# A mixture-of-experts feed-forward in one core: the first product by a seven-multiplication block scheme, with the hidden rows written to memory and read back by a second phase

## What is computed

```python
h = jax.lax.ragged_dot(x_rep_sort, w1, group_sizes)
h = jax.nn.silu(h) * jax.lax.ragged_dot(x_rep_sort, w3, group_sizes)
out_sort = jax.lax.ragged_dot(h, w2, group_sizes)
...
out = jnp.einsum('tkd,tk->td', out_rep, topk_w)
return out.reshape(b, s, d)
```

## Time and profile before

| | |
|---|---|
| three timed runs | 8394.23, 8397.29, 8398.87 us (median 8397.29) |
| profiled execution | 8408.29 us, its span 8406.7 us |
| PE busy | 8220.8 us, 98% |
| DVE busy | 3531.5 us, 42% |
| ACT busy | 3267.5 us, 39% |
| POOL busy | 478.6 us, 6% |
| bytes moved | 1189.77 MB, 142 GB/s over the span |

### The profile page before, as it was taken

How to read it: one execution, slowest core, us unless ns; L and a number is a source line. 1 busy time by engine, 2 the same in 40 slices (tenths; PEclk the granted TensorE clock), 3 DMA queues, 4 the chain that set the end, 5 groups by cost and what they waited for, 6 DMA issues and landing times.

```text
span 8406.7 us, 119512 instructions
## 1 busy us (share of the span) xinstructions
PE 8220.8 (98%) x46092; PEld 7566.7 (90%) x46093; DVE 3531.5 (42%) x3602; ACT 3267.5 (39%) x3511; POOL 478.6 (6%) x580
## 2 busy tenths in 40 slices
PE   8959999999999999999999999999999999999998
PEld 5549999999999999999999999999999999999998
DVE  6755333443443334453333334453333334433343
ACT  2325333443333334453333334453333333433343
POOL 2320000000000000000000000000000000000000
PEclk8969999999999999999999999999999999999999
DMA  3335444553443434553434434554434344444343
GB/s 113 115 111 185 142 135 135 179 162 131 139 149 122 147 120 151 169 185 120 141 129 134 141 128 150 161 187 142 135 130 139 120 145 141 152 143 135 130 154 116
DMA packets 839095, 1189.77 MB, mean 142 GB/s; under 512 B 27872, under 2 KB 722400, under 8 KB 839072
## 3 DMA queue, kind: packets, MB, share of 16 engines
q1 hardware_dynamic: 812096, 1116.05, 40.5%
q0 software_dynamic: 26976, 73.42, 3.7%
HBM read 1121.90 MB, written 71.67 MB: 142 GB/s over the span
## 4 chain that ended last, share of the span: by engine, by line
PE 92%; ACT 0%; issue 0%; DVE 0%; DMA 0%; ACTq 0%; POOL 0%; POOLq 0%; DVEq 0%
PE p L1038 20%; PE p L1040 20%; PE p L1039 20%; PE acc L1063 10%; PE acc L1064 10%; PE acc L1062 10%; PE p L1093 1%; DVE lo L975 0%; ACT hi L921 0%; ACT L921 0%; DMA out_x<-y,id_s 0%; DMA xg<-x_rows,id_g 0%; DVE xlo L1001 0%; ACT xhi L946 0%; ACT y L963 0%
## 5 line engine op out<-in xcount | busy, mean ns | idle before, releaser
L1038 PE MATMUL p<-xhi,hi 128*128 128x384 f32 (+4 forms) x10752 | 3435.3, 320 | 30.6 <-DVE lo L975 19.1
L1040 PE MATMUL p<-xhi,lo 128*128 128x384 f32 (+4 forms) x10752 | 3432.7, 319 | 0.0
L1039 PE MATMUL p<-xlo,hi 128*128 128x384 f32 (+4 forms) x10752 | 3430.0, 319 | 0.0
L1038 PEld LDWEIGHTS p<-xhi,hi 128*128 128x128 f32 x10752 | 2029.1, 189 | 65.7 <-issue 41.3
L1039 PEld LDWEIGHTS p<-xlo,hi 128*128 128x128 f32 x10752 | 2030.5, 189 | 24.3
L1040 PEld LDWEIGHTS p<-xhi,lo 128*128 128x128 f32 x10752 | 2028.1, 189 | 0.0
L988 DVE TENSOR_TENSOR hid<-sil,p 128x384 f32<-128x384 f32 x672 | 372.4, 554 | 3764.0 <-PE p L1040 3764.0
L975 DVE TENSOR_TENSOR lo<-raw,hi 128x2048 fp32r<-128x2048 f32 x673 | 1543.4, 2293 | 792.8 <-ACT hi L921 792.8
L1062 PE MATMUL acc<-hi,hhi 128*128 128x512 f32 x3808 | 1497.6, 393 | 0.0
L1064 PE MATMUL acc<-hi,hlo 128*128 128x512 f32 x3808 | 1491.5, 392 | 0.0
L1063 PE MATMUL acc<-lo,hhi 128*128 128x512 f32 x3808 | 1490.6, 391 | 0.0
(11 more groups left out here) (181 smaller groups left out, 2439.4 us busy)
## 6 DMA issues: line engine op xcount, KB each, us to landing
raw<-in_L_ffn_w SPq DMA_DIRECT2D x1011, 1024.0 KB, 5.1
xin<-in_x SPq DMA_DIRECT2D x8, 2048.0 KB, 10.7
out_x<-x SPq DMA_DIRECT2D x32, 512.0 KB, 2.9
x_rows<-x SPq DMA_DIRECT2D x32, 512.0 KB, 3.7
ctxt<-in_ctx SPq DMA_DIRECT2D x4, 1024.0 KB, 9.6
table<-rec,posi POOLq DMA_INDIRECT x80
xg<-x_rows,id_g POOLq DMA_INDIRECT x75, 6.7
out_x<-y,id_s POOLq DMA_INDIRECT x72, 7.3
```

What stands on the lines that cost most here:

```text
L1038: pe.matmul(bank[:, 0:n], hi13[par][:, a, k, :], xhi[:, k, 0:n], start=(k == 0), stop=False)
L1039: pe.matmul(bank[:, 0:n], hi13[par][:, a, k, :], xlo[:, k, 0:n], start=False, stop=False)
L1040: mm = pe.matmul(bank[:, 0:n], lo13[par][:, a, k, :], xhi[:, k, 0:n], start=False, stop=(k == KT - 1))
```

## The change

`experts` is rewritten. A slot is now up to 1024 rows of one expert (HALF = 512), cut into an even half and an odd half of equal width n; n is rounded up to one of WIDTHS. An expert whose count needs an odd number of 512s starts with a slot of 512 rows. With the counts above there are 12 slots: two with n = 496, two with n = 512, and eight narrow ones (experts 2, 4, 6 and 7 have two each): four with n = 256, three with 272, one with 288.

**First phase.** 28 units per slot: a unit is one matrix (w1, then w3) for two tiles of hidden columns. Cut in 2 by 2 blocks (two tiles by two halves of k, and two halves of k by two halves of the rows), it takes seven products instead of eight, each of 4 steps of k with three matmuls of n columns: 84 matmuls. For that, four sums of weight blocks are formed by POOL for every unit (`weight_sums`, into `sums`), four sums of row blocks once per slot (`row_sums`), and DVE combines the products from four banks into four results (`unit`), since the banks are used again within the unit. ACT and DVE split seven weight operands of 512 columns per unit (`weight_hi`, `weight_lo`). The hidden values of a pair go to a tensor `hd` in memory (1 MB per pair of tiles).

**Second phase.** After the 28 units, four passes c over the 28 tiles: one half of the rows (nh) by one half of the output columns (dh). Here w2 is stationary and the hidden values are moving, n columns at a time. A step is two tiles: SP loads 512 KB of w2 and 512 KB of `hd`, ACT and DVE split both, PE does 24 matmuls. 56 steps per slot; w2 and `hd` are read twice each in this way. Between steps t+5 and t+6 of a pass PE turns the results of the pass before back (`turn_back`, 16 transposes) and turns a quarter of the next slot's rows (`turn_rows`, 16 transposes). ACT, DVE and POOL have the copies for these in their queues.

In narrow slots ACT and DVE work on 288 columns (NARROW) where they otherwise work on 512. `raw13[1]` serves in the second phase as the second buffer of w2 and `hd`.

The diff, cut to its core:

```diff
+HALF = 512
+KH = KT // 2
+EP = 7
+PAIRS = MT // 2
+UNITS2 = 2 * PAIRS
+WIDTHS = (256, 272, 288, 384, 496, 512)
+NARROW = 288
...
-                sp.wait_ge(s_lo13, s * MT + pair * 2 - 1)
-                sp.dma_start(raw13[parity][:, 0], w1v[bass.ds(e, 1), :, :, bass.ds(pair * 2 * P, 2 * P)].rearrange(
...
+            def load_down(e, c, i, par):
+
+                nh, dh = c // 2, c % 2
+                sp.dma_start(raw2[par], w2v[bass.ds(e, 1), :, bass.ds(i * 2, 2), dh * HALF:(dh + 1) * HALF].rearrange(
+                    "e p m d -> (e p) m d")).then_inc(s_raw2[par], 16)
+                sp.dma_start(rawh[par], hdv[nh, :, bass.ds(i * 2, 2), :]).then_inc(s_rawh[par], 16)
+
+            def store_hidden(s, i):
+
+                sp.wait_ge(s_hid, s * (PAIRS * 3) + i * 3 + 3)
+                sp.dma_start(hd[bass.ds(i * 4, 4)].rearrange("q p n -> p q n"), hid[:, :, :]).then_inc(s_hst, 16)
...
+                                sp.wait_ge(s_w2lo, s * STEPS + c * PAIRS + i2 * 2 + par + 1)
+                                sp.wait_ge(s_hlo, s * STEPS + c * PAIRS + i2 * 2 + par + 1)
+                                load_down(e, c, i2 * 2 + par, par)
...
+            def down_hi(s, t, cols):
+
+                par = t % 2
...
+                act.wait_ge(s_down, s * (STEPS * 4) + 4 * t + 4)
+                act.wait_ge(s_raw2[par], s * (STEPS * 8) + (t // 2) * 16 + 16)
+                copy(wh[:, 4 * par:4 * par + 2, :], raw2[par]).then_inc(s_w2hi, 1)
+                act.wait_ge(s_rawh[par], s * (STEPS * 8) + (t // 2) * 16 + 16)
+                copy(wh[:, 4 * par + 2:4 * par + 4, 0:cols], rawh[par][:, :, 0:cols]).then_inc(s_hhi, 1)
...
+                after(3)
+                product_done(s, i, a, 4)
+                plus(v[:, 0:cols], s1[:, 0:cols], b2[:, 0:cols]).then_inc(s_v, 1)
+                dve.wait_ge(s_v, g + 2)
+                plus(to[:, 3, 0:cols], v[:, 0:cols], b4[:, 0:cols]).then_inc(s_c22, 1)
+                after(4)
+                if a == 1:
+                    dve.wait_ge(s_c22, g + 1)
+                    gate(3, 1)
+                product_done(s, i, a, 5)
+                plus(to[:, 1, 0:cols], v[:, 0:cols], b5[:, 0:cols]).then_inc(s_c12, 1)
+                after(5)
+                if a == 1:
+                    dve.wait_ge(s_c12, g + 2)
+                    gate(1, 2)
+                product_done(s, i, a, 6)
+                dve.wait_ge(s_u2, g + 1)
+                plus(to[:, 2, 0:cols], u2[:, 0:cols], b4[:, 0:cols]).then_inc(s_c21, 1)
+                after(6)
...
+                    for k in range(KH):
+                        ks = slice(k * P, (k + 1) * P)
+                        pe.matmul(o, wh[:, e, ks], xh[:, e, k, 0:n], start=begin and k == 0, stop=False,
+                                  skip_group_check=True)
+                        pe.matmul(o, wh[:, e, ks], xl[:, e, k, 0:n], start=False, stop=False, skip_group_check=True)
+                        mm = pe.matmul(o, wl[:, e, ks], xh[:, e, k, 0:n], start=False, stop=k == KH - 1,
+                                       skip_group_check=True)
...
+                pe.wait_ge(s_c11, g + 1)
+                product(0, b1, True)
+                pe.wait_ge(s_c21, g + 1)
+                product(1, b4, True)
+                pe.wait_ge(s_v, g + 1)
+                product(2, b2, True)
+                pe.wait_ge(s_s1, g + 1)
+                product(3, b1, False)
+                pe.wait_ge(s_u2, g + 1)
+                product(4, b2, False)
+                pe.wait_ge(s_c12, g + 1)
+                product(5, b5, True)
+                pe.wait_ge(s_c22, g + 1)
+                product(6, b4, False)
...
+                free(1)
+                G.tensor_tensor(sums[:, 0, :, :], A11, A21, ALU.subtract).then_inc(s_sum, 1)
+                free(4)
+                G.tensor_tensor(sums[:, 1, :, :], A21, A22, ALU.add).then_inc(s_sum, 1)
+                pool.wait_ge(s_sum, done + 2)
+                free(2)
+                G.tensor_tensor(sums[:, 2, :, :], sums[:, 1, :, :], A11, ALU.subtract).then_inc(s_sum, 1)
+                pool.wait_ge(s_sum, done + 3)
+                free(5)
+                G.tensor_tensor(sums[:, 3, :, :], A12, sums[:, 2, :, :], ALU.subtract).then_inc(s_sum, 1)
```

More of the change, by code:

```diff
@@ L697, in by_slot @@
                 return a[0:1, :].unsqueeze(1).to_broadcast([1, META, E])
-            s_i, mine, i_in, start, t_a, t_b = (sl[:, i, :, :] for i in range(6))
+            s_i, mine, start, t_a, t_b = (sl[:, i, :, :] for i in range(5))
             step(V.tensor_copy(s_i, sidx[:, :, :]))
@@ new lines, in copy, with weight_hi @@
+            def copy(out, in_, scale=1.0):
+                return nc.scalar.activation(out, in_, ACT.Copy, scale=scale)
+            def weight_hi(s, i, a, e, fresh=False, first=False):
+                if first:
+                    pass
+                elif fresh:
+                    act.wait_ge(s_down, s * (STEPS * 4) + (4 if e < 4 else 8))
+                else:
+                    act.wait_ge(s_prod, s * PRODUCTS + i * (2 * EP) + a * EP + e + 1)
+                if e == 0:
+                    act.wait_ge(s_raw13[a], s * (PAIRS * 16) + i * 16 + 16)
+                if e in SUM_OF:
+                    act.wait_ge(s_sum, s * (PAIRS * 8) + i * 8 + a * 4 + SUM_OF[e] + 1)
+                copy(by_k(wh[:, e, :]), weight_part(a, e)).then_inc(s_whi, 1)
@@ new lines, in quad, with rows_hi @@
+            def quad(n, q, first=False):
+                act.wait_ge(s_xt, n * 4 + q + 1)
+                if not first:
+                    act.wait_ge(s_xlo, n * EP)
+                copy(quads[:, q, :, :], by_k(bank[q][:, :])).then_inc(s_quad, 1)
+            def rows_hi(n, c, i):
+                e, q, ready = X_PARTS[i]
+                if ready:
+                    act.wait_ge(s_xsum, n * 4 + ready)
+                else:
+                    act.wait_ge(s_quad, n * 4 + q + 1)
+                copy(xh[:, e, :, c * P:(c + 1) * P], quads[:, q, :, :]).then_inc(s_xhi, 1)
@@ new lines, in _ @@
+            act.wait_ge(s_clear, 1)
+            for e in range(EP):
+                weight_hi(0, 0, 0, e, first=True)
+            for c in range(4):
+                if c == 0:
+                    act.wait_ge(s_wlo, EP)
+                for q in range(4):
+                    quad(c, q, first=c == 0)
+                for i in range(EP):
+                    rows_hi(c, c, i)
+            with act.Fori(0, SLOTS) as s:
+                width = slot_value(act, 2, s, N8_MOST)
+                with act.If(width > 0):
+                    with act.If(width > NARROW // 8):
+                        slot(s, HALF)
+                    with act.Else():
+                        slot(s, NARROW)
+                    act.nop()
@@ new lines, in _ @@
+            dve.wait_ge(s_raw13[0], 16)
+            less(sums[:, 0, :, :], A11, A21).then_inc(s_sum, 1)
+            plus(sums[:, 1, :, :], A21, A22).then_inc(s_sum, 1)
+            dve.wait_ge(s_sum, 2)
+            less(sums[:, 2, :, :], sums[:, 1, :, :], A11).then_inc(s_sum, 1)
+            dve.wait_ge(s_sum, 3)
+            less(sums[:, 3, :, :], A12, sums[:, 2, :, :]).then_inc(s_sum, 1)
+            for e in range(EP):
+                weight_lo(0, 0, 0, e)
+            for c in range(4):
+                for i in range(EP):
+                    rows_lo(c, c, i)
@@ L1055, in hidden @@
[L1055 removed]
+                        between(lo, half)
+                between(0, len(WIDTHS) - 1)
                 pe.nop()
[L1058 to L1064 removed]
@@ L1205, in moe_kernel @@
+            tick(0)
+            for c in range(4):
+                gather(c, first_x[2 * c:2 * c + 2], s_xfirst[c])
+            for c in range(4):
+                row_sums(c)
+            pool.wait_ge(s_xlo, 4 * EP)
+            weight_sums(0, 0, 1)
+            with pool.Fori(0, SLOTS) as s:
+                width = slot_value(pool, 2, s, N8_MOST)
+                with pool.If(width > 0):
+                    slot(s, width)
+                pool.nop()
 def moe_kernel(nc, x, ctx_in, W_k, b_k, gamma, beta, gate_w, w1, w2, w3, out):
```

864 lines of the change are left out of this document (546 added, 318 removed).

## The result

The changed kernel takes **9136 us** (median of 4 runs, 9135.2 to 9146.3), the kernel before 8398 in the same session: a ratio of **1.088**, 95% interval 1.086 to 1.090. It is slower, as forecast, but by 8.8% and not by 1.4%: the time lies outside of the range of 8060 to 8950.

What follows compares the result with a forecast made beforehand. PE's matmuls were taken to bound the kernel. Span 8407 - 694 + 159 + 22 = 7894, plus 254 (first phase), 276 (second phase) and 100 (clock) = 8524; forecast 8515 us, 1.4% slower, range 8060 to 8950.

Steps and rivals of the forecast that it cites:

- PE's work, minus 694: PE's matmuls in both phases: first phase 623 us less, second phase 72 us less.
- First phase, DVE and POOL, plus 254: Narrow first-phase units: DVE and POOL delay each other, so PE waits; 234 us narrow, 20 wide, at 1.1 us per sum.
- the exclusion: First phase: DVE operations with both inputs in SBUF and POOL's sums block each other; 234 us in narrow slots.
- Second phase, plus 276: Second-phase loads: 3.4 us per step against PE's 2.9 in narrow slots; 260 us narrow, 16 wide, range 0 to 736.
- Clock, plus 100: PE's granted clock falls after pauses, with 60 seams and many short waits; 100 us, range 0 to 250.
- Seams, plus 159: Transposes and waits between steps and at slot ends: 22 us per slot, 264 in all, for 105 before.
- start, plus 22: Kernel start: 1024 rows to gather, turn, sum and split before the first product; 22 us on top of 39.
- The covers hold: Faster rival: DVE and POOL do not hold each other up, loads keep pace; about 8060 us, chance 0.25.
- POOL's sum at IOTA's rate: Slower rival: first-phase POOL sums of 2.1 us make narrow units 13.8 us; around 9000 us, chance 0.11.
- The loads collide: Slower rival: second-phase loads delay each other, 4.3 us per step, DMA share above 0.9; 9000 us, chance 0.05.

Runs made afterwards that it cites:

- e1: Changed kernel with POOL's four weight sums per unit working on one element instead of 512 (stale sums, waits kept); 8848 us, 1.053.
- e16: e13 with high parts first in the first phase too (8648 us), and DVE's two weight sums moved to the start of the unit before; 8504 us.
- e9: Changed kernel with SP's waits parted in the second phase: w2 and hidden-row loads each wait only for their own half of the buffer; 9034 us.
- e2: Changed kernel with SP issuing second-phase loads of steps 2 to 7 before waiting for the last hidden store and loading next weights; 9054 us.
- e13: e12 with PE's eight high-part products first in each second-phase step, then the sixteen with low parts; 8650 us, 1.029.
- e3: Changed kernel with PE's code built for two slot widths (288, 512) instead of six; 9184 us, 1.093.
- e15: e13 with high parts first in the first phase too, weight and row sums cut to one element (stale), none on DVE; 8263 us, 0.983.
- e18: e16 with PE's code for four widths (256, 272, 288, 512) instead of three, nothing left out; 8443 us, 1.005.
- e12: Changed kernel with loads first, narrow hidden loads, three widths, parted waits, third second-phase load buffer, weight sums shared by POOL and DVE; 8774 us.

## Why the prediction was right or wrong, point by point

- **PE's work, minus 694: right.** 28,224 and 16,128 matmuls, at the distances of the earlier trace rows; wide first phases at 530 to 535 us.
- **First phase, DVE and POOL, plus 254: the mechanism right, the term incomplete.** For the exclusion the text had 36, 24 and 17 us a phase at 256, 272 and 288 columns, 234 in all; e1 gives 37, 30 and 29, 266 in all, a part of which may be the chain that e16 mends. A sum takes 1.44 to 1.56 us beside DVE, not 1.1. The Trainium skill's rule that the second to issue waits ("SBUF — State Buffer", Who interferes with whom) now has a row for a long POOL operation, L1176 at 1.54. What failed is that nothing else stretches a narrow first phase in the sum: there are 40 us of pauses at the ends of the eight phases, and the chain of load, POOL and DVE (e16: 144 us, in its arrangement). A narrow phase of 256 columns was to be 320 and is 344.
- **Second phase, plus 276: failed, and the largest part of the miss.** The step that failed is the round through a load's buffer. The text put it at 6.8 us, 3.4 per step: a load, then ACT's copy and DVE's difference of the last part alone (0.69 and 0.75); what it names adds up to 6.2. One round in the trace after, from one issue for a buffer to the next, shows more:

```profile
2803.09 0.37 SPq L939 DMA_DIRECT2D raw<-in_L_ffn_w  x1
...
2807.17 1.06 ACT L980 ACTIVATE wh<-raw 128x1024 fp32r<-128x1024 f32 x1 [1.82 <-DMA raw<-in_L_ffn_w]
...
2808.26 1.89 DVE L1153 TENSOR_TENSOR wl<-raw,wh 128x1024 fp32r<-128x1024 f32 x2 [1.90 <-ACT wh L980]
...
2810.49 0.37 SPq L939 DMA_DIRECT2D raw<-in_L_ffn_w  x1
```

It is the weight's half that comes last: 4.1 us for its load, ACT's 1.06 on it, both differences of DVE in a row (1.89), and 0.3 to the next issue, 7.4 us. The median over the narrow slots is 8.0. Steps that nothing else disturbs take 3.8 us instead of 3.4, and passes 63 to 69 instead of 58. Parting SP's waits takes the second difference out of the round (e9: 102 us). Nor was SP's queue order followed past the last store: a wait of 9 us and 1 MB stand ahead of step 2 (e2: 83 us), for which no term was there. Behind the round through the load's buffer lies one through PE's operands (e13: 124 us). The text also has a slip: at 3.15 us per step a pass is 14 x 3.15 + 10 = 54, not 53, and the excess 221 us, not 180.
- **Pauses for code: missing.** 137 us of pauses, in no term and no rival; 12 are left with two widths (e3). The changed kernel has six bodies of 84 and of 48 matmuls for PE under branches, 792 matmuls. The kernel before has bodies by width too, five of 48, twice (L1047 to L1055), 480 matmuls for the first product, and the earlier trace rows show 0% of issue: the forecast needed the number of bodies, not only that there are some.
- **Clock, plus 100: too small.** In narrow phases the distances of matmuls with no idle time between them exceed those of the earlier trace rows by 209 us in all (235 with the wide ones), at a granted clock of 0.89 to 0.93 in narrow second phases. It is smaller where PE waits less: in e15, by the same count, 80 us.
- **Seams, plus 159, and start, plus 22: near.** Wide second phases of e18, 332.6 us with the SP order mended, lie 4 us above 614/2 + 22; the start is 10 us shorter.
- **The rivals.** "The covers hold" fell in both terms. "POOL's sum at IOTA's rate", decided above 1.4 us per sum, names the right side, and the sum is at that point; but narrow units last 12.2 us, not 13.8, and e1 bounds all of POOL's weight sums by 288 us. "The loads collide" wanted a DMA share above 0.9; it is 0.73, and e9 raised it to 0.81 while the phase got shorter. So 9136 is near the price of two rivals and has the cause of neither, but half a dozen causes of 70 to 290 us each.
- **The shape of the error.** The span is 610 us over the forecast's 8524. By the counts above, second phases' waits are 285 of them (561 for 276), pauses 137 (for nothing), the clock 135 (235 for 100) and first phases 63 (317 for 254), less 10 at the start. Each cover was costed against one partner. The range took in wrong sizes of the two terms but no third and fourth term.

## What to carry to other kernels

When a change takes an engine from 98% busy to thin cover, write down every round that passes through a buffer (load, split, split, multiply, free) with its waits as the code has them, and the order of the queue that refills it, before costing any single operation: here the rounds and the queue were worth more than the operation that had been suspected. Measure a scheme's floor with its added work cut to nothing early; it tells in one run whether mending the rest can pay. Count the bodies of code that a loop by cases makes for one engine, and round sizes up to fewer cases if that keeps its code small.

## What the runs showed of the hardware

- PE's instructions come in packets of 16 KB. With bodies for three or four widths 12 or 13 packets were fetched in the run, with five 18, with six 85; PE's pauses at changes of phase, with five and six widths, lasted 3.4 to 16.7 us.
- DVE's operations with two inputs in SBUF are held up by POOL's additions: 512 columns take 889 ns on average beside POOL's sums and 689 without them; one of 288 columns, 451 without, took 1.54 us and ended 0.31 us after POOL's. One with an input in PSUM (288 columns) stays at 447 to 452 ns.
- POOL's addition of 512 elements per partition takes 1.26 us at the least and 1.44 to 1.56 on average beside DVE.
- A 512 KB load of weights beside the others lands in 4.1 to 4.7 us (medians). The load of hidden rows takes 5.0 at 512 KB and 4.3 at 288 KB: in this range its time is mostly not its bytes.

The last but one shows in e12's line of POOL's third sum (duration ns min/median/max):

```profile
L1553 POOL TENSOR_TENSOR sums<-sums,raw x25: 1260/1532/2165, 615.4 to 8758.7; 128x512 f32<-128x512 f32 x25
```
